# GNN kernel, edge stage: destination rows gathered onto the source rows by adding indirect DMAs

## What is computed

```python
h = jnp.concatenate([n_embed[senders], n_embed[receivers]], axis=-1)   # 2 x 256
h = jnp.tanh(h @ W0 + b0)            # 406 wide, padded to 416
h = jnp.tanh(h @ W1 + b1)            # 323 wide, padded to 324
h = h @ W2 + b2
h = h * (e_embed @ Wg)
return _segment_mean(h, senders, n_embed.shape[0])
```

## Time and profile before

| what | value |
|---|---|
| timed, median of 3 | 3271.17 us |
| span of the profiled execution | 3707.1 us, 13% over the median; no other time of its own is listed |
| table stage (0 to 132 us of the span) | 132 us |
| edge stage (132 to 2158 us) | 2026 us |
| node stages (2158 to 3707 us) | 1549 us |
| TensorE, VectorE, ScalarE, GpSimd busy | 89%, 58%, 43%, 37% of the span |

### The profile page before, as it was taken

The page is one execution under the profiler, slowest core; times in us unless marked ns, Lnnn a source line. Parts: engine busy times, 40 slices in busy tenths (PEclk is TensorE's granted clock), DMA queues, the critical chain, the costliest instruction groups (busy, mean ns, idle before and its releaser), DMA issues. The chain is left out here.

```text
span 3707.1 us, 68629 instructions
## 1 busy us (share of the span) xinstructions
PE 3298.7 (89%) x19277; PEld 2783.2 (75%) x19278; DVE 2156.1 (58%) x5404; ACT 1576.1 (43%) x3210; POOL 1363.5 (37%) x1410
## 2 busy tenths in 40 slices
PE   7688888888888888888888889899999999999999
PEld 6466766777767666767676766777888999999888
DVE  7566666666666665666666668899444211124422
ACT  2344545554555444555454547777111111111244
POOL 2556666666666555666665422222000000000000
PEclk9799999999999999999999989999999999999999
DMA  4444444444444433444444368888755666666465
GB/s 159 138 124 129 129 129 130 136 132 126 134 133 134 124 119 118 129 132 132 135 125 120 97 190 254 253 263 264 228 176 176 205 210 211 205 218 203 144 206 163
DMA packets 288343, 605.46 MB, mean 163 GB/s; under 512 B 38577, under 2 KB 195850, under 8 KB 288266
## 3 DMA queue, kind: packets, MB, share of 16 engines
q1 hardware_dynamic: 170848, 321.14, 28.0%
q0 software_dynamic: 73216, 232.67, 20.7%
q10 hardware_dynamic: 44202, 50.63, 4.0%
HBM read 493.97 MB, written 110.32 MB: 163 GB/s over the span
## 5 line engine op out<-in xcount | busy, mean ns | idle before, releaser
L998 PE MATMUL bank<-ring,parts 128*128 128x320 f32 x4000 | 641.6, 316 | 5.4 <-issue 2.5
L998 PEld LDWEIGHTS bank<-ring,parts 128*128 128x128 f32 x4000 | 595.1, 188 | 16.3 <-issue 10.9
L679 PE MATMUL bank<-w2h,hidden2h 108*128 108x256 f32 x1248 | 421.0, 337 | 143.1 <-DVE rows_out L906 112.0
L624 POOL DMA_INDIRECT msgs<-rows_out,sidx x416 | 427.5, 1028 | 306.9 <-PE bank L712 157.4
L617 POOL DMA_INDIRECT p_in<-p_tab,gidx x416 | 402.1, 967 | 289.2 <-issue 125.6
L617 POOL DMA_INDIRECT q_in<-q_tab,gidx x416 | 408.7, 982 | 231.3 <-issue 116.1
L679 PE MATMUL bank<-hidden1h,w1h 128*108 128x512 f32 x936 | 422.1, 451 | 23.7 <-DVE hidden2l L867 22.0
L679 PEld LDWEIGHTS bank<-w2h,hidden2h 108*128 108x128 f32 x1248 | 248.6, 199 | 194.0 <-DVE rows_out L906 142.4
L680 PE MATMUL bank<-hidden1l,w1h 128*108 128x512 f32 x936 | 382.6, 409 | 0.1
L681 PE MATMUL bank<-hidden1h,w1l 128*108 128x512 f32 x936 | 380.0, 406 | 0.0
L681 PE MATMUL bank<-w2h,hidden2l 108*128 108x256 f32 x1248 | 366.1, 293 | 4.2 <-issue 4.1
(11 more groups left out here) (243 smaller groups left out, 6137.6 us busy)
## 6 DMA issues: line engine op xcount, KB each, us to landing
ring<-counts SPq DMA_DIRECT2D x250, 800.0 KB, 4.3
R_buf<-msgs SPq DMA_DIRECT2D x544, 130.0 KB, 3.0
counts<-cells ACTq DMA_DIRECT2D x125, 320.0 KB, 3.4
eT<-in_edge_T SPq DMA_DIRECT2D x104, 256.0 KB
p_in<-p_tab,gidx POOLq DMA_INDIRECT x416
q_in<-q_tab,gidx POOLq DMA_INDIRECT x416
msgs<-rows_out,sidx POOLq DMA_INDIRECT x416
p_tab<-p_out SPq DMA_DIRECT2D x25, 208.0 KB, 1.9
```

What stands on the lines that cost most here:

```text
L624: pool.indirect_dma_start(out=msgs[:], in_=rows_out[:, z, c], in_offset=None, out_offset=bass.IndirectOffsetOnAxis(ap=sidx[:, z, c:c + 1], ...
L679: pe.matmul(out, lh.bitcast(F32R), rh.bitcast(F32R), start=first, stop=False)
L998: mm = pe.matmul(banks[q][:, 0:NW], part[:, TB * i + a, h * P:(h + 1) * P].bitcast(dt), ring[:, slot, a].bitcast(dt), start=first and x == ...
```

## The change

Destination rows are no longer gathered into a buffer of their own. `gather` brings the `p` rows of group t+2 straight into `pre1`, and `gather_onto` brings the `q` rows onto the same place with a DMA that adds (`compute_op=ALU.add`). It waits until the `p` rows of its tile have landed. VectorE's `add`, `p_in`, `q_in` and `s_add` are gone. TensorE waits for the rows' own semaphores. The tables hold the last 32 columns three times (`H1W` = 480 columns in place of 416), made by the weights' layout; the fourth transposed block is 96 wide in place of 128. Where `p` rows were gathered three groups ahead it is now two: they wait for the transposes of group t (`s_T`), which frees their slot. The index copy (`next_rows`) on VectorE stands once a body and waits for the four tiles of group t+1.

```diff
-        p_tab, q_tab = dram("p_tab", [NP, H1]), dram("q_tab", [NP, H1])
+        p_tab, q_tab = dram("p_tab", [NP, H1W]), dram("q_tab", [NP, H1W])
...
-            p_in, q_in = (esb(n, [P, 2, GC, H1]) for n in ("p_in", "q_in"))
-            pre1 = R_buf[:, 0:2 * GC * H1T * P].rearrange("p (z c n) -> p z c n", z=2, c=GC)
+            pre1 = esb("pre1", [P, 2, GC, H1W])
...
+                def gather(t, c):
+                    z = t.slot(2)
+                    pool.indirect_dma_start(out=pre1[:, z, c], out_offset=None, in_=p_tab[:],
+                                            in_offset=bass.IndirectOffsetOnAxis(ap=gidx[:, z, 0, c:c + 1], axis=0)
                                             ).then_inc(s_in_rows[z][c], 16)
+                def gather_onto(t, c):
+                    z = t.slot(2)
+                    pool.wait_ge(s_in_rows[z][c], 32 * t.use(2) + 16)
+                    stand_alone(pool, s_up)
+                    pool.indirect_dma_start(out=pre1[:, z, c], out_offset=None, in_=q_tab[:],
+                                            in_offset=bass.IndirectOffsetOnAxis(ap=gidx[:, z, 1, c:c + 1], axis=0),
+                                            compute_op=ALU.add).then_inc(s_in_rows[z][c], 16)
...
-                    if t.has(3):
-                        pool.wait_ge(s_idx, t.group(3) + 1)
-                        wait(pool, s_add, (t.group(3) - 1) * GC)
+                    if t.has(2):
+                        pool.wait_ge(s_idx, t.group(2) + 1)
+                        wait(pool, s_T, (t.group(0) + 1) * GC)
...
-                    pe.wait_ge(s_add, j * GC + c + 1)
+                    pe.wait_ge(s_in_rows[z][c], 32 * (t.use(1) + 1))
...
-                    for k in range(H1T):
-                        mm = pe.transpose(bT[c % 2][:, k * C:(k + 1) * C], pre1[:, z, c, k * P:(k + 1) * P], ident[:])
-                    mm.then_inc(s_T, 1)
+                    for k in range(H1F):
+                        pe.transpose(bT[c % 2][:, k * C:(k + 1) * C], pre1[:, z, c, k * P:(k + 1) * P], ident[:])
+                    pe.transpose(bT[c % 2][0:H1Q, H1F * C:], pre1[:, z, c, H1F * P:], ident[:]).then_inc(s_T, 1)
...
-                def add(t, c):
-                    v.wait_ge(s_in_rows[z][c], 32 * (t.use(2) + 1))
-                    wait(v, s_T, (j - 2) * GC + c + 1)
-                    if c == GC - 1 and t.has(4):
-                        table_rows(z, t.group(4))
+                def next_rows(t):
+                    z = t.slot(3)
+                    if t.has(1):
+                        for c in range(GC):
+                            v.wait_ge(s_in_rows[z][c], 32 * (t.use(1) + 1))
+                    table_rows(z, t.group(3))
```

More of the change, by code:

```diff
@@ L40 @@
 H1T, H1Q = H1F + 1, 3 * H1R
+H1W = H1F * P + H1Q
 LOW = slice(2 * H1R, H1Q)
@@ L562, in build @@
             s_eT = [esem(f"s_eT{z}") for z in range(2)]
-            s_idx, s_add, s_T, s_th1, s_lo1 = (esem(n) for n in ("s_idx", "s_add", "s_T", "s_th1", "s_lo1"))
+            s_idx, s_T, s_th1, s_lo1 = (esem(n) for n in ("s_idx", "s_T", "s_th1", "s_lo1"))
             s_L1, s_th2, s_lo2, s_L2, s_gt, s_msg = (esem(n) for n in ("s_L1", "s_th2", "s_lo2", "s_L2", "s_gt", "s_msg"))
@@ L640, in body @@
                         stand_alone(pool, s_up)
-                    if t.has(3):
+                    if t.has(2):
                         for c in range(GC):
-                            gather(t, c, q_tab, 1, q_in)
+                            gather_onto(t, c)
                     ending = isinstance(t.it, int) and t.group(0) >= G
@@ L656, in body @@
                             scatter(t, c)
-                edge_loop(pool, body, -3, 4, G - 4, G + 2)
+                edge_loop(pool, body, -2, 4, G - 4, G + 2)
                 for z in range(2):
@@ L754, in body @@
                     places_after(t)
+                pe.wait_ge(s_one, 2)
                 edge_loop(pe, body, -1, 3, G - 1, G + 1)
@@ L822, in table_rows @@
                     v.tensor_copy(gidx[:, z], edge_i[:, :, at]).then_inc(s_idx, 1)
-                def add(t, c):
-                    j, z = t.group(2), t.slot(2)
-                    if not t.has(2):
+                def next_rows(t):
+                    if not t.has(3):
                         return
-                    v.wait_ge(s_in_rows[z][c], 32 * (t.use(2) + 1))
-                    wait(v, s_T, (j - 2) * GC + c + 1)
-                    if c == GC - 1 and t.has(4):
-                        table_rows(z, t.group(4))
-                    full, rest = slice(0, H1F * P), slice(H1F * P, H1)
-                    v.tensor_tensor(pre1[:, z, c, full], p_in[:, z, c, full], q_in[:, z, c, full], ALU.add)
-                    copies = [P, P // H1R, H1R]
-                    v.tensor_tensor(pre1[:, z, c, H1F * P:].rearrange("p (r n) -> p r n", n=H1R),
-                                    p_in[:, z, c, rest].unsqueeze(1).broadcast_to(copies),
-                                    q_in[:, z, c, rest].unsqueeze(1).broadcast_to(copies), ALU.add
-                                    ).then_inc(s_add, 1)
+                    z = t.slot(3)
[3 more added lines that the diff above has]
+                    table_rows(z, t.group(3))
                 def first_low(t, c):
@@ L912, in body @@
                     first_low(t, 1)
-                    add(t, 0)
                     second_low(t, 0)
@@ L916, in body @@
                     first_low(t, 2)
-                    add(t, 1)
                     second_low(t, 1)
                     first_low(t, 3)
-                    add(t, 2)
+                    next_rows(t)
                     message(t, 0)
                     message(t, 1)
-                    add(t, 3)
                     second_low(t, 2)
@@ L929, in _ @@
                     table_rows(z, z)
+                for unused in bT:
+                    v.memset(unused[H1Q:P, H1F * C:], 0.0).then_inc(s_one, 1)
                 v.memset(hidden2h[:], 1.0).then_inc(s_one, 1)
@@ L932, in _ @@
                 v.tensor_copy(count_to, iota[:, 0:P]).then_inc(s_one, 1)
-                v.wait_ge(s_one, 3)
-                edge_loop(v, body, -2, 3, G - 5, G + 1)
+                v.wait_ge(s_one, 5)
+                edge_loop(v, body, -1, 3, G - 3, G + 1)
                 v.wait_ge(s_next, G)
@@ L1788, with widened @@
     xp = padded(np.asarray(x), (NP, D))
-    W0 = padded(w["L0_gnn_W0"], (2 * D, H1))
+    def widened(a):
+        rest = a[:, H1F * P:]
+        return np.concatenate([a, rest, rest], axis=1)
+    W0 = widened(padded(w["L0_gnn_W0"], (2 * D, H1)))
     W1 = padded(w["L0_gnn_W1"], (H1, H2))
```

28 lines of the change are left out of this document (12 added, 16 removed).

## The result

| kernel | median us | ratio to before |
|---|---|---|
| before | 3270.13 (3268.99 to 3275.09) | 1 |
| after | 3512.14 (3510.58 to 3515.65) | 1.0736, 95% interval 1.0723 to 1.0749 |

The changed kernel is 242 us slower. It was forecast at 3465 us, inside 3310 to 3660. Its profiled execution took 3511.93 us, so its trace can be read against the median as it stands.

A forecast was written before the change was run, and what follows sets the result against it. TensorE and GpSimd were taken to bound the edge stage together, 15.29 us a group when timed. Adding gathers bring GpSimd to 17.1: 3271 + 6 (tables) + 188 (building) = 3465 us, range 3310 to 3660.

The forecast's parts named there:

- What bounds before: Edge stage: TensorE 15.23 and GpSimd 15.2 us a group need the same time; 15.29 when timed.
- Adds leave VectorE: Edge stage: VectorE is relieved of 3.4 us a group but is not the bound; 0 to 6 us off.
- Table stage: Its 300 matmuls get 480 columns in place of 416: +6 us, between 0 and 13.8.
- Building: GpSimd's queue: each adding q gather takes 0.48 us more to build, 1.9 us a group, +188 us over 104 groups.
- The pages' estimate: GpSimd's queue: read side's work doubles, each q gather costs up to 0.9 us more, sum near +382 us.
- The waits: GpSimd's waits for p rows before adding gathers are covered, 1.5 us to spare: 0.
- Two groups ahead: Edge loop: adding gathers of group t+2 land before TensorE wants them at 15 us: 0.
- transposes: TensorE: the same 16 a group, same streamed width, the last of each tile 96 columns narrow: 0.
- Transfers: Edge stage's DMA queues: 362 MB on the software queue, 1292 us with the hardware queue, under 1590 us, so hidden.
- Rival 1: GpSimd: building an adding DMA costs nothing more; time stays 3271 us. Chance 0.17.
- Rival 2: Edge stage: the adds were in TensorE's way, so their removal makes it faster, 3237 us. Chance 0.17.
- Rival 3: Edge stage: adding transfers (about +300 us, 3575) or four waits for landing (+333 us) slow it. Chance 0.16.

The follow-up runs named there:

- e2: Changed kernel with adding q gathers for tiles 0 and 1 of a group only, copying ones for 2 and 3; 3397.99 us, ratio 1.0387.
- e3: Changed kernel with adding q gathers of half a row, 240 of the 480 columns, same number of rows; 3508.67 us, ratio 1.0722.
- e4: Changed kernel with GpSimd waiting for all four tiles' p rows before the first adding gather; 3849.64 us, ratio 1.1767.
- e5: Kernel before with a thirteenth DMA a group, a second copying gather of tile 0's q rows into an unread buffer; 3430.49 us, ratio 1.0488.
- e6: Kernel before with its q gathers adding onto q_in, cleared once, VectorE's adds kept; 3550.74 us, ratio 1.0850.
- e9: Changed kernel with adding gathers for 64 of the 128 partitions; 3454.78 us, ratio 1.0563.
- e7: Kernel before with q gathers for tiles 0 and 1 only, their rows also serving tiles 2 and 3; 3270.18 us, ratio 0.9997.
- e1: Changed kernel with q gathers that copy over the p rows, all else of the change kept; 3268.53 us, ratio 0.9987.
- e8: Kernel before, unchanged, run again for a second profile; 3271.16 us, span 3269.4.
- e12: Changed kernel with adding gathers for 8 of the 128 partitions; 3731.3 us beside 3753.71 for before, ratio 0.9948.
- e10: Changed kernel with copying q gathers for 64 of the 128 partitions; 3794.87 us beside 3766.3 for before on its chip.

## Why the prediction was right

The theory's sum against the runs on chips where before takes 3271 us:

| | GpSimd's sum, us a group | step of the first one-hots | time by the sum | measured |
|---|---|---|---|---|
| after | 17.58 | 17.57 | 3515 | 3512 |
| e2 | 16.46 | 16.45 | 3399 | 3398 |
| e3 | 17.59 | 17.55 | 3516 | 3509 |
| e4 | 20.8 | 20.81 | 3850 | 3850 |
| e5 | 16.78 | 16.74 | 3428 | 3430 |
| e6 | 17.9 | 17.85 | 3545 | 3551 |
| e9 | 17.09 | 17.04 | 3464 | 3455 |
| e7 (copying, ten DMAs) | 13.0 | 15.24 | TensorE's floor | 3270 |
| e1 (copying, twelve) | 15.15 | 15.23 | TensorE's floor | 3269 |

- **What bounds before.** Right. The prediction took 436 us off the first profile's edge stage and got 15.29 us a group; e8 shows 15.27. Taking all of it from this stage was a choice. By the first one-hots of the groups it was: the first profile has 2003.7 us from the first (132.3) to the last (2136.0) where e8 has 1572.8, 431 more, and 5 us more behind them. Wrong was the name given to the stretch: the prediction took the late releases as the profiler's, but e8 and the profiled executions of e1 to e7 and e9 take what their kernels' other runs take, within 0.2%.
- **Adds leave VectorE: 0 to 6 us off.** Right: e1 is 3.2 us under before by medians (0.04% to 0.23% by the interval), its wide tables paid for.
- **Table stage: +6 us** (0 to 13.8). The first p gather starts at 115.08 us in place of e8's 107.20, 7.9 later, so the wide tables themselves cost slightly more than forecast. At the first one-hot only 4.3 are left, and in e1 1.5: without the adds on VectorE the loop fills faster, which the prediction didn't count.
- **Building: +0.48 us each, +188 us.** The step is right and its size too small: +0.59 us (1.551 - 0.962). GpSimd's sum goes from 15.25 to 17.58 us a group, of which 17.58 - 15.27 = 2.31 show; 103 steps make 238 us, of 236.9 measured. The value lay within the bounds 0 and 0.95, above their middle. The reason given for the middle was wrong in its form: I argued per row (a row's reading described twice, its writing once); the runs show a price that is mostly per DMA. That 0.48 came within 0.11 us of the measured value is luck so far as it rests on that reason.
- **The pages' estimate.** The Trainium skill (Collectives: The Full Stack, "The bandwidth ceiling: the fold count and why AG ≠ RS ≠ AR", with the GPSIMD Engine Reference, "When to use GPSIMD") gave an extra of up to 0.9 us by doubling the read side's descriptors. Measured: 0.59 us. From 128 to 8 rows the packets of an adding gather fall from 144 to 32 and its time to build only from 1.551 to 1.342 us. If packets follow the descriptors, which no run shows, most of the price does not scale with them; the trace does not bear the estimate out.
- **The waits: 0.** Right: gap 0.30 us in front of the adding gathers, and e1, which keeps them, loses nothing. The landing of a p gather takes 3.6 us (page) against 3.5 forecast and 5.0 of cover. e4 shows that the cover was worth 3.2 us a group.
- **Two groups ahead, transposes: 0.** Right by e1.
- **Transfers: hidden.** Right: e3 moves 51 MB of q rows less on the software queue (208.81 in place of 259.93 in the whole execution) and gains under 4 us; the software queue's 63.3% of 1858 us are 1176 us, 1197 forecast. Its bytes are not the 362 MB forecast: the profile counts 259.93 MB with and without adding. The price of the adding shows in its time, 33.9% of 3510.2 us in place of e1's 26.5% of 3268.3, 324 us more.
- **Rival 1** (building costs nothing more) fell with the 1551 ns. **Rival 2** (faster, adds in TensorE's way): its waits of 207 us were a mark of the stretched execution, 1.6 us in e8. Its contention is real but small, and it was absent from the p gathers of before: between 200 and 1700 us of e8 they take 0.96 us in the mean with or without an add beside them for over 0.3 us, though single ones take up to 1.32, and the q gathers 0.97 against 0.95. In e5 and e6 the p gathers with an add beside them take 1.08 to 1.09 us and the others 0.97. By the Trainium skill (SBUF — State Buffer, "Who interferes with whom") a VectorE instruction with two SBUF inputs contends with a GpSimd instruction that reads SBUF; the trace agrees in e5 and e6, at 0.06 us a p gather over all of them. **Rival 3** did not occur; e4 shows what a wait for landing would have cost.
- **Slips in its sums.** 4 x 0.1 to 4 x 0.95 us a group are +32 to +386 us without the table stage's 6 and +38 to +392 with it. Four times 0.9 us on top of 15.2 are +365 us over 15.29, 371 with the tables, where the pages' estimate says 382. Rival 1 counts 3 us for the tables where the forecast counts 6. From 5 us into the body, at 1.25 us each and 3.5 to landing, the adding gathers land at 8.5 to 12.3 us and not at 10 to 14. None of them decides anything.

## What to carry to other kernels

When two engines need the same time for a turn of the loop, work moved from a third one onto either of them lengthens the turn: sum each engine's turn, gaps in front of its DMAs included, before moving it. Letting a DMA add is not free where GpSimd builds it: 0.59 us more for each here, mostly whatever the number of its rows, so it pays only where GpSimd has that room. When a profiled execution is far from the timed runs, subtract, say from which stage, and take a second profile before reading its waits.

## What the runs showed of the hardware

- An adding indirect gather of 128 rows takes GpSimd 1.551 us to build (after), a copying one 0.945 (e1); an adding one 1.342 even for 8 rows (e12), and 1.551 for rows of 960 and of 1920 bytes (e3, after).
- An adding gather of 128 rows shows as 144 packets, a copying one as 64; the bytes counted are the same (e1, after).
- An adding gather of 1920-byte rows lands 5.4 us after its issue, one of 960-byte rows 3.7 (e3), a copying one of 1920 bytes 3.6.
- GpSimd's gap between DMAs that wait for nothing is 0.30 us, and a wait that is already over adds nothing to it (0.30 at 1019.19 in the changed kernel).
- TensorE's granted clock was 1.00 where it was busy for 1558 of 1560 us (e1, e8) and 0.97 in the changed kernel's edge stage, where it waits 1.6 us a group; the clock is then a consequence, since GpSimd's sum alone gives the time.
- The same program took 3271 us on three chips and 3719 to 3829 us on two. There engines are released late: ScalarE's waits put down to "remote" in front of its first tanh (L770) are 252 us in e10, and GpSimd's in front of its q gathers 145, by the trace from 140 to 1700 us; e8 has no such wait there. Its cause is open.
